# Inverse W transform as three rounded products instead of one f32 product, with the rounding done at the inverse H evictions and POOL taking copies and subtractions

## What is computed

```python
B, H, W, C = (4, 128, 128, 768)
xf = jnp.fft.rfft2(x.astype(jnp.float32), axes=(1, 2), norm='ortho')
...
o1r = jax.nn.relu(jnp.einsum('bhwni,nio->bhwno', xr, w1[0]) - jnp.einsum('bhwni,nio->bhwno', xi, w1[1]) + b1[0])
o1i = jax.nn.relu(jnp.einsum('bhwni,nio->bhwno', xi, w1[0]) + jnp.einsum('bhwni,nio->bhwno', xr, w1[1]) + b1[1])
o2r = jnp.einsum('bhwno,noi->bhwni', o1r, w2[0]) - jnp.einsum('bhwno,noi->bhwni', o1i, w2[1]) + b2[0]
o2i = jnp.einsum('bhwno,noi->bhwni', o1i, w2[0]) + jnp.einsum('bhwno,noi->bhwni', o1r, w2[1]) + b2[1]
o2r = softshrink(o2r, LAMBD)
o2i = softshrink(o2i, LAMBD)
...
out = jnp.fft.irfft2(xc, s=(H, W), axes=(1, 2), norm='ortho').astype(dtype)
return out + bias        # bias is x
```

## Time and profile before

| what | value |
|---|---|
| time, median of 3 runs (lowest to highest) | 5124.27 us (5121.58 to 5125.56) |
| span of the profiled execution | 5120.9 us |
| granted TensorE clock, mean | 0.999 of full speed |
| busy: PE, DVE, ACT, POOL | 98%, 78%, 49%, 12% |
| one block, from the rows of one to the rows of the next | 157 to 161 us |

### The profile page before, as it was taken

The page is one execution under the profiler, slowest core; times in us unless marked ns, Lnnn a source line. Parts: engine busy times, 40 slices in busy tenths (PEclk is TensorE's granted clock), DMA queues, the critical chain, the costliest instruction groups (busy, mean ns, idle before and its releaser), DMA issues.

```text
span 5120.9 us, 112005 instructions
## 1 busy us (share of the span) xinstructions
PE 5023.2 (98%) x43200; PEld 4143.8 (81%) x43200; DVE 3992.9 (78%) x5987; ACT 2512.6 (49%) x3649; POOL 626.9 (12%) x420
## 2 busy tenths in 40 slices
PE   7999999999999999999999999999999999999999
PEld 6887878878788887888888888888878878888887
DVE  6778778787787877878777777777787777877877
ACT  4554545545455454554445544545545455454553
POOL 0111011110111101111011110011110111101111
PEclk9999999999999999999999999999999999999999
DMA  3331233312333123332133321333312333123311
GB/s 108 100 102 34 74 101 100 105 44 61 100 100 105 51 55 100 100 105 62 46 98 100 105 77 45 83 100 105 91 44 71 100 105 99 44 63 100 104 51 50
DMA packets 1067748, 421.11 MB, mean 82 GB/s; under 512 B 1064864, under 2 KB 1064992, under 8 KB 1067168
## 3 DMA queue, kind: packets, MB, share of 16 engines
q1 hardware_dynamic: 1062432, 411.63, 30.4%
q10 hardware_dynamic: 4736, 1.60, 0.1%
HBM read 210.26 MB, written 201.33 MB: 80 GB/s over the span
## 4 chain that ended last, share of the span: by engine, by line
issue 88%; POOL 12%; POOLq 0%; DVE 0%
POOL x L948 12%; POOLq L947 0%; POOLq L951 0%; DVE x L877 0%; POOLq L948 0%; POOLq L960 0%
## 5 line engine op out<-in xcount | busy, mean ns | idle before, releaser
L948 POOL TENSOR_TENSOR x<-shrink_or_v,x 128x480 f32<-128x480 f32 (+1 forms) x416 | 626.7, 1506 | 4485.8 <-DVE shrink_or_v L870 4445.1
L549 PE MATMUL ps<-wts,hbig 128*128 128x192 f32 x4160 | 732.1, 327 | 4.3
L842 DVE TENSOR_TENSOR shrink_or_v<-ps,wts 128x768 f32<-128x768 f32 (+1 forms) x544 | 501.1, 921 | 285.3 <-PE ps L558 258.6
L795 DVE COPY ydg<-ps 128x512 f32<-128x512 f32 (+5 forms) x768 | 504.7, 657 | 251.4 <-PE ps L453 151.7
L453 PE MATMUL ps<-tab,ring 128*128 128x128 f32 x6144 | 694.6, 276 | 4.2
L453 PEld LDWEIGHTS ps<-tab,ring 128*128 128x128 f32 x6144 | 688.5, 192 | 10.3 <-DVE ring L916 10.3
L549 PEld LDWEIGHTS ps<-wts,hbig 128*128 128x128 f32 x4160 | 673.2, 190 | 16.3 <-ACT hbig L710 13.7
L440 PE MATMUL ps<-tab,ring 128*64 128x128 f32 x6144 | 680.4, 273 | 3.3 <-ACT ring L650 3.3
L660 ACT COPY ydg<-ps 127x512 f32<-127x512 f32 (+5 forms) x896 | 503.0, 571 | 361.6 <-PE ps L453 185.3
L441 PE MATMUL ps<-tab,ring 128*63 128x128 f32 x6144 | 680.4, 273 | 0.0
L440 PEld LDWEIGHTS ps<-tab,ring 128*64 128x64 f32 x6144 | 671.3, 137 | 7.9 <-ACT ring L650 4.8
(11 more groups left out here) (79 smaller groups left out, 7581.0 us busy)
## 6 DMA issues: line engine op xcount, KB each, us to landing
out<-x SPq DMA_DIRECT2D x352, 480.0 KB, 4.6
x<-in_x SPq DMA_DIRECT2D x192, 768.0 KB, 7.6
x<-in_x SPq DMA_DIRECT2D x32, 816.0 KB, 7.8
x<-in_x SPq DMA_DIRECT2D x32, 720.0 KB, 6.4
out<-x SPq DMA_DIRECT2D x32, 432.0 KB, 4.2
wts<-in_mix SPq DMA_DIRECT2D x16, 513.0 KB, 3.6
out<-x SPq DMA_DIRECT2D x32, 240.0 KB, 4.4
out<-x SPq DMA_DIRECT2D x32, 192.0 KB, 4.3
```

The source lines that it names most:

```text
L549: mm = pe.matmul(o, hbig[:, k * H:(k + 1) * H], mix_part("w2_big"), start=first, stop=False, skip_group_check=True)
L795: dve.tensor_copy(*line_moves(stage, g)).then_inc(line_dve, 1)
L842: dve.tensor_tensor(parts(v), d, b2, ALU.add).then_inc(bias_done, 1)
L948: pool.tensor_tensor(xs[p][:, a:b, :], ucopy[g % 4][:, 0:b - a, :], mirror(xs[p], a, b), ALU.add).then_inc(plus_ready, 1)
```

## The change

- The four matrices' halves `odd_hi`, `odd_lo`, `even_hi`, `even_lo` are made once at the start: `hi` is the matrix rounded to `fp32r`, `lo` what is left.
- The result of the inverse lines is kept in two forms from row position 20 on (`HEAD`): rounded (`yhi`, in the place of `ydg`) and the remainder (`ylo`). Positions 0 to 19 stay f32 in `ydg`.
- The moves of the inverse lines go by *units* of two groups (groups 22 to 25 singly): ACT copies the head (20 positions) and then the tail (108 positions, rounding), DVE subtracts `tail - yhi` into `ylo`. Before, ACT and DVE each moved every second group alone.
- The packs of the inverse lines are shared anew: ACT groups 0 to 4, 10, 16, 22; DVE the other odd ones; POOL the other even ones (6, 8, 12, 14, 18, 20, 24), each with a one-element multiply ahead of it.
- All odd products of the rows, and the even ones from group 4 on, become three `fp32r` products. The even products of groups 0 to 3 stay f32.
- Subtractions of the groups 5, 7, 9 and 11 go from DVE to POOL, behind POOL's addition of the same group. `ucopy` now has a place for every group, so `add_halves` no longer waits for the subtraction four groups before.
- SBUF is laid out anew: buffers of the mixing share one area with `ylo` and `ucopy`, and the low half of the first layer's weights lies over the weights. ACT's first copy of a block's mixing waits for POOL's and DVE's last use of that area.

```diff
 def packer_h(g):
-    return "act" if g < RING or g % 3 == 2 else "dve"
+    if g < RING or g in (10, 16, 22):
+        return "act"
+    return "dve" if g % 2 else "pool"
...
+UNITS = [(g, g + 1) for g in range(0, 22, 2)] + [(g,) for g in range(22, NG)]
...
+PLAIN = 4
+HEAD = HG * PLAIN
+TAIL = H - HEAD
+POOL_MINUS = (5, 7, 9, 11)
...
+        def wait_unit(engine, q, g):
+
+            engine.wait_ge(head_moved, NUNITS * q + UNIT_OF[g] + 1)
+            engine.wait_ge(lo_moved, NUNITS * q + UNIT_OF[g] + 1)
...
+        def unit_parts(i):
+
+            unit = UNITS[i]
+            c, n = LINE_GROUPS[unit[0]]
+            bank, n = line_bank(1, unit[0]), n * len(unit)
+            d = ps[:, bank:bank + len(unit), 0:n * 128 // len(unit)].rearrange("p b (c k) -> p k (b c)", k=128)
+            return slice(c, c + n), d[:, 0:HEAD], d[:, HEAD:H]
...
                 def inverse_lines(q):
                     for g in range(NG):
                         if g >= 8:
-                            wait_moved(pe, q, 1, g - 8)
+                            wait_unit(pe, q, g - 8)
...
+                def split_rows(o, hi, lo, a, b, cols):
+
+                    yh, yl = yhi[:, a:b, cols], ylo[:, a - HEAD:b - HEAD, cols]
+                    pe.matmul(o, lo, yh, start=True, stop=False)
+                    pe.matmul(o, hi, yh, start=False, stop=False)
+                    return pe.matmul(o, hi, yl, start=False, stop=True)
...
+                def even_part(q, g, cols):
+                    o = ps[:, row_bank(g), 0:HG * CB].rearrange("p (h c) -> p h c", c=CB)[:, :, cols]
+                    a, b = HG * g, HG * g + HG
+                    if g < PLAIN:
+                        return pe.matmul(o, mat("inv_w_even"), ydg[:, a:b, cols], start=True, stop=True)
+                    return split_rows(o, even_hi[:], even_lo[:], a, b, cols)
...
+                def inverse_lines(q):
+                    for g in range(NG):
+                        n = g + RING
+                        if n < NG and packer_h(n) == "act":
+                            pack(q, n)
+                        if g == UNITS[UNIT_OF[g]][-1]:
+                            cols, head, tail = unit_parts(UNIT_OF[g])
+                            act.wait_ge(line_done, lines_before(q, 1, g) + 1)
+                            act.copy(ydg[:, 0:HEAD, cols], head).then_inc(head_moved, 1)
+                            act.copy(yhi[:, HEAD:H, cols], tail).then_inc(hi_moved, 1)
...
+                        if g == UNITS[UNIT_OF[g]][-1]:
+                            cols, _, tail = unit_parts(UNIT_OF[g])
+                            dve.wait_ge(hi_moved, NUNITS * q + UNIT_OF[g] + 1)
+                            dve.tensor_tensor(ylo[:, :, cols], tail, yhi[:, HEAD:H, cols],
+                                              ALU.subtract).then_inc(lo_moved, 1)
...
                         for g in range(NF + 2):
                             if g < NF:
                                 add_halves(q, p, g)
-                            if g >= 2:
+                            if g >= 2 and g - 2 not in POOL_MINUS:
                                 subtract(q, p, g - 2)
...
+                def pack(q, g):
+                    pool.wait_ge(line_seen, PACKED_H["pool"] * q + upto(packer_h, g, "pool"))
+                    pool.wait_ge(line_done, lines_before(q, 1, g - RING) + 1)
+                    pool.tensor_tensor(turn[:], turn[:], turn[:], ALU.mult).then_inc(line_seen, 1)
+                    pool.tensor_copy(*pack_moves(g)).then_inc(packed_pool, 1)
...
                         for g in range(NF):
...
+                            add(q, p, g)
+                            if g in POOL_MINUS:
+                                subtract(q, p, g)
```

More of the change, by code:

```diff
@@ L42, in packer_h, with mover @@
 def packer_h(g):
-    return "act" if g < RING or g % 3 == 2 else "dve"
-def mover(stage, g):
-    if stage == 0 and g < 4:
+    if g < RING or g in (10, 16, 22):
         return "act"
-    return "dve" if g % 2 else "act"
+    return "dve" if g % 2 else "pool"
+def mover(g):
+    return "dve" if g >= 4 and g % 2 else "act"
 def upto(owner, g, who):
@@ L56 @@
 PACKED_A = {who: upto(packer_a, NG - 1, who) for who in ("act", "dve")}
[L57 to L58 removed]
+PACKED_H = {who: upto(packer_h, NG - 1, who) for who in ("act", "dve", "pool")}
+MOVED = {who: upto(mover, NG - 1, who) for who in ("act", "dve")}
+UNITS = [(g, g + 1) for g in range(0, 22, 2)] + [(g,) for g in range(22, NG)]
+NUNITS = len(UNITS)
+UNIT_OF = {g: i for i, unit in enumerate(UNITS) for g in unit}
 GROUP_PAIRS = ([[(6, 7), (8, 9), (10, 11), (12, 13)], [(0, 64), (14, 15), (16, 17), (18, 19)]]
@@ L186, in sem, with base, over @@
             return ctx.enter_context(nc.semaphore(name))
+        def base():
+            return -(-nc.sbuf_base // 32) * 32
+        def over(name, shape, dt, at, words):
+            return nc.alloc_sbuf_tensor_at(name, shape, dt, offset=at + 4 * words)
+        area = base()
+        sb("area", [128, TAIL * CB])
+        ylo = over("ylo", [128, TAIL, CB], F32R, area, 0)
+        ucopy = over("ucopy", [128, TAIL, CB], F32, area, 0)
+        zbig = [over(f"zbig{j}", [128, 8 * H], F32, area, 8 * H * j) for j in range(2)]
@@ L190, in build @@
         ydg = sb("ydg", [128, 128, CB])
+        yhi = over("yhi", [128, 128, CB], F32R, y_at, 0)
         yedge = sb("yedge", [128, 4, CB])
         row0 = sb("row0", [128, CB])
+        turn = sb("turn", [1, 1])
+        ring = [sb(f"ring{j}", [128, CG, 128]) for j in range(RING)]
+        w1hi = sb("w1hi", [128, 3 * BIG], F32R)
+        wts_at = base()
         wts = sb("wts", [128, MIXED])
-        zbig = [sb(f"zbig{j}", [128, 8 * H]) for j in range(2)]
-        zhi = sb("zhi", [128, 8 * H], F32R)
@@ L207, in build @@
[L207 to L211, removed]
+        w1lo = over("w1lo", [128, MIXED], F32R, wts_at, 0)
         ps = ctx.enter_context(nc.psum_tensor("ps", [128, 8, 512], F32))
@@ L295, in lines_before, with moved_count, wait_moved, batch_of @@
             return 2 * NG * q + stage * NG + g
[L297 to L304, removed]
-            c, n = LINE_GROUPS[g]
-            rows = 127 if stage == 0 else 128
-            return (ydg[0:rows, :, c:c + n],
-                    ps[0:rows, line_bank(stage, g), 0:n * 128].rearrange("p (c k) -> p k c", c=n))
+        def moved_count(q, g, who):
+            return MOVED[who] * q + upto(mover, g, who)
+        def wait_moved(engine, q, g):
+            who = mover(g)
+            engine.wait_ge(line_sems[who], moved_count(q, g, who))
+        def batch_of(g):
+            return next(i for i, last in enumerate(STORE_AFTER) if g <= last)
+        def batch_part(g):
+            return 2 if g == NF - 1 else 1
+        def wait_batch(engine, q, g):
+            engine.wait_ge(batch_ready[batch_of(g)], 2 * q + 4)
+        def wait_unit(engine, q, g):
+            engine.wait_ge(head_moved, NUNITS * q + UNIT_OF[g] + 1)
+            engine.wait_ge(lo_moved, NUNITS * q + UNIT_OF[g] + 1)
+        def line_moves(g):
+            c, n = LINE_GROUPS[g]
+            return (ydg[0:127, :, c:c + n],
+                    ps[0:127, line_bank(0, g), 0:n * 128].rearrange("p (c k) -> p k c", c=n))
+        def unit_parts(i):
[4 more added lines that the diff above has]
+            return slice(c, c + n), d[:, 0:HEAD], d[:, HEAD:H]
+        def ucopy_of(g):
+            a, b = odd_rows(g)
+            return ydg[:, a:b, :] if g < PLAIN else ucopy[:, a - HEAD:b - HEAD, :]
         def fold_rows(i):
```

184 lines of the change are left out of this document (107 added, 77 removed).

## The result

The changed kernel takes 5182.05 us (median of 4 runs, 5180.73 to 5191.81) against 5124.92 us beside it: ratio 1.0115, 95% interval 1.0103 to 1.0127. It is 1.1% slower; 5168 was forecast, in a range of 5060 to 5230.

What follows compares the result with a forecast made beforehand. PE, 98% busy, was taken as the bound, with forward group 7's pack the narrowest place. +1.3 us a block over 31 passages (+40) and some +3 at the end made the span 5164, forecast 5168 us, range 5060 to 5230.

Steps and rivals of the forecast that it cites:

- What bounds the kernel now: Whole kernel: PE, busy 98% of the span; narrowest place DVE's pack of forward group 7, 1.5 us to spare.
- Part 1: Rows on PE: rounded products of 480 columns take 0.216 us each, saving 3.0 us a block.
- Part 2: Inverse lines: moves and packs hidden, but their end makes group 0 about 0.5 us later, range 0.2 to 1.0.
- Part 3: Rows stage: POOL's twelve operations end at 24.2 us; PE may begin forward group 7 at 25.4 against 24.6.
- The sum: Per block: +0.5 from the inverse lines' end and +0.8 from the rows stage, +1.3 us; PE's 3.0 inside the wait.
- the last block's +2.9: End of the program: the last block ends with POOL and DVE and adds 0.5 + 2.4, some +3 us.
- B: Rival: POOL's operations in a row are cheaper than alone, some of PE's gain kept; 5050 to 5113 us, chance 0.23.
- C: Rival: PE's saving arrives in full bar 0.5 us, DVE not late at group 7; 5030 to 5050, chance 0.07.
- E: Rival: the clock falls in PE's new waits, +30 to +60 us on top; 5230 and beyond, chance 0.06.

Runs made afterwards that it cites:

- The cut at 80 channels: The changed kernel with the first rows cut at 80 channels instead of 88: 5185.2 us, ratio 1.0128 to the kernel before.

## Why the prediction was right

**What bounds the kernel now.** Right. Forward group 7's pack, behind DVE's last subtraction, behind POOL's last addition, was the narrowest place. Taking the four subtractions off POOL gave back 42 of 57 us; taking two thirds of the products away gave 24, though with the clock at its lower level for much of the rows stage.

**Part 1.** Right in size: 480 rounded columns every 0.216 us, rows to row 0 shorter by 2.7 us inside a turn (3.0 minus the wait for `add_halves(9)`).

**Part 2.** The inverse lines themselves are hidden, as said: PE has no new wait in them, their last line starts at the same place (23.1 us behind the merge copy in both kernels), and POOL's pack, bounded at 0.6 to 2.4, takes 1.10 us. Their end was mis-sized: +0.5 forecast, +1.0 measured (32.8 / 32). Both terms of it were too small. The rows begin 0.7 us later than before (23.9 instead of 23.2 us behind the merge copy; 0.45 forecast), of which the profile shows 0.52 as PE's wait. And group 0 takes 1.99 us (2100.20 to 2102.19) instead of 1.69 (2074.74 to 2076.43), +0.3 where +0.15 was forecast. Half of that is the even product of 440 columns: from its start to the next product's it takes 0.88 us, and took 0.74 before:

```profile
2075.33 0.90 PE L596 MATMUL ps<-ydg,tab 128*128 128x440 f32 x2
2076.07 0.30 PE L598 MATMUL ps<-ydg,tab 128*128 128x32 f32 x2
```

The product has not changed; what follows it has. The remainders of the small units end in DVE at 2101.50 (2099.04 + 2.46), and the narrow part starts at 2101.64:

```profile
2099.04 2.46 DVE L899 TENSOR_TENSOR ylo<-ps,yhi 128x864 fp32r<-128x864 f32 x5 [0.22 <-ACT yhi L751]
```

The cut at 80 channels agrees: the small units' chain ends the stage in any case.

**Part 3.** Right term by term. Twelve operations in a row were forecast from 8.1 to 24.2 us, 16.1 us; they ran from 7.8 (2111.10) to 23.8 (2127.13 on a clock that starts at 2103.34), 16.0 us. An addition takes 1.2 and a subtraction 1.5, and the 0.3 is what was forecast for a DVE subtraction beside it: each of POOL's four begins while one of DVE's is under way, and the one that began with none beside it, the last in the run with two operations exchanged, took 1.20. What was not in my sum is the other side, DVE's blocked subtractions (1.65 us). They changed little, since DVE then waits for POOL anyway, but they are why the exchange of two operations gave nothing.

**The sum** for a passage was +0.8 and came out as +0.68 inside a turn and +1.11 across: 16 x 0.68 + 15 x 1.11 = 27.5 us of medians, 32.9 by the means (forecast 25). The difference between the two is the four passages inside a turn in which the clock fell behind the wait at group 7, 1.6 us each. Only the passages inside a turn are the mechanism that was forecast. In the 15 across, PE is not held by the pack but comes late by the loop's return and the lower clock, neither of which is in the sum; that they cost about as much as the forecast's term is luck. The run with four blocks in a turn shows that the pack would have held PE in 8 of them too, at nearly the same price. The end of the inverse lines gave 32.8 (forecast 16), mixing gave back 6.9, and the last block's +2.9 didn't come (-0.3). So 5168 was 14 us low: 17 us are the term of part 2, and the other misses, +8 in the passages, -7 in mixing, -3 at the end and +1 at the start, nearly cancel.

**The rivals.** B and C needed POOL at 1.1 us or less; it was at 1.2. E was half there: the clock falls in 19 passages to a half for 3.4 us, PE's products of the forward lines are busy 35.8 us longer (716.2 us in L507 against 680.4 in L440 before), but mostly in place of the wait for the pack. And 15 of the 19 fell behind another wait than the one forecast; behind the wait of 2.4 us at group 7 it stayed at 1.00 in 12 of 16.

## What to carry to other kernels

Work taken off the busiest engine is worth only as much as the first thing that then comes late; here it was found by putting the handover between two stages on one clock and asking which instruction stands last in each engine's order before the next stage's first need. Operations moved to POOL count at their full length in a row, and a VectorE operation with two SBUF inputs that is issued while one of them runs is blocked until that one ends (0.65 us became 1.65 here), so test such a move by the end of POOL's chain and not by POOL's share of the span. When an engine gets faster in front of its loop's return, the return can become the next wait; lengthening the loop's body to eight blocks was worth 7 us in the kernel before and 36 us in the changed one with its subtractions back on DVE, while with POOL's chain still in the way a body of four blocks was worth nothing.

## What was unexpected of the hardware

- PE's loop return costs 0.4 us a passage before and shows once PE is early: in the changed kernel the row-0 matmul came 3.1 us after the last product's start in the passages across the return, 0.6 us in the others. The number of such waits followed the number of returns: 15, 7 and 3. What takes the time within the return wasn't tried.
- Blocking between POOL and DVE goes by who begins first: 0.33 us lost by POOL in the earlier trace rows, 1.0 us lost by DVE in the changed kernel, on the same kind of pair of two-input operations.
- The granted clock fell to 1.2 GHz behind 15 of 15 waits of 2.7 to 2.8 us ahead of row 0, behind 4 of 16 waits of 2.4 us at group 7, and in the run with a fourth product behind 6 of 15 waits of 1.8 to 2.0 us ahead of row 0. A fall cost 1.6 us in the forward lines.
- POOL copies 512 strided columns from SBUF in 1.10 us, as fast as ACT (1.09).
